# Pair products from tile 2 on, dense sums in place, six tile buffers in a ring, and two waits moved: one change to a fused attention and feed-forward kernel

## The chip, the cores and the metric

The kernel runs on one core of one Trainium2 chip. TensorE (PE) does the matmuls, VectorE (DVE), ScalarE (ACT) and GpSimd (POOL) the rest; SyncE (SP) issues nearly all transfers and POOL a few, and 16 DMA engines carry them. The metric is device time in microseconds for one execution; the output is checked against the reference, and smaller is better.

## The reference, cut to what matters

```python
x = L0_attn_inputs                       # (2, 1024, 1024), float32
x = x + attention(layernorm(x))          # conv of 3 taps to q, k, v (256 each), 16 heads of 64,
                                         # causal softmax in blocks of 128, wo, proj_w, proj_b
x = x + ffn(layernorm(x))

def ffn(x):                              # 2048 tokens, H = O = 1024, rank 8, 4 active experts of 16
    y = einsum('bth,oh->bto', x, W_base) + b_base
    z = einsum('bth,erh->bter', x, lora_A[active])
    contribs = einsum('bter,eor->bteo', z, lora_B[active]) * 2.0
    logits = (einsum('bth,eh->bte', x, router_W) + router_b)[..., active]
    alpha = softmax(log(domain_prior[active] + 1e-12) + logits)
    return y + einsum('bteo,bte->bto', contribs, alpha)
```

## The kernel before

It is one program in which each engine's instructions stand in an order written by hand, with semaphores between them. Every float32 product is done as three matmuls on a high and a low part (`three_pass`, L63 to L65). There are three stages: the convolution, the attention and the feed-forward part.

**Attention.** The 2048 tokens go in 8 groups of 256, each in 8 steps of two heads; two of these steps make one `attention_pair(D)`, so D runs from 0 to 32 and a group takes four of them. In pair D, TensorE does the scores of pair D-1, the head outputs of D-3, the turning of the softmax rows of D-2 (L1882, which waits for `p_ready`), and then queries and keys of D (at the start of a group these wait for `c_lo_ready`). GpSimd normalises the softmax rows (L722, which gives `p_ready`) and makes `c_lo` (L703); in every fourth pair it first adds the bias row to the residual rows `xr` (`bias_sum`, L713). The queries and keys come from `c_raw`, one buffer into which SP loads a group of 256 tokens (`load_c`, L480), and which ACT (`c_high`, L920) and GpSimd empty. SP issues transfers in the order of `attention_step(g, i)`: in step (0, 0) it gathers the gate weights of the four active experts (the list, then for each expert a register load and four small transfers, L607 to L614), in (0, 7) it loads group 2 of `c_raw`, in (1, 0) it loads the dense weights `fw_raw` (24 transfers, L618), and in (1, 3) the bias row `pb_r` and the first `xr`.

**Feed-forward.** 16 tiles of 128 tokens. The first `CL` = 4 are done plainly: `dense(t, b)` runs 8 chunks x 3 passes over three column blocks (1064 columns in all, 36 of them for gates and low rank), then three short matmuls add the low-rank part from `b_stack` (L2088), and DVE adds the sum to the tile's residual `x1t` and writes it to a buffer `y` of its own (`tile_outputs`, L1612), which POOL stores. The other 12 tiles go in 6 pairs of two tiles: seven products of half size in place of eight (`product`, L2039 to L2041, by the operands A11, S1, S2, A12, S3, A22, S4). Three of them use sums of weight blocks. These were formed in the attention stage, stored to memory, and come back in the feed-forward stage (`load_sums(kind)`, L567): kinds 0, 1 and 2 (each 8 transfers of 266 KB, into `t_v`, `t_p`, `t_b`, `t_f`) are for S1, S2 and S3, and kind 3 (8 of 266 KB into the right halves of `fw_hi` and `fw_lo`) is for A22. Kind 3 may only be loaded once the last plain tile is done with those columns (`y_done`), and each product's first matmul waits for its kind.

**Buffers.** Six buffers `x1t_0` to `x1t_5` hold residual tiles. `x1t_4` and `x1t_5` lie where `y` lies, so they are free only once the plain tiles are stored; `x_slot(t)` says which tile has which buffer. `x1g` holds a second, group-wise copy of a tile for its normalised and transposed operand (`load_groups(t)`, L539, four transfers of 128 KB, waits for `fturned`). Before the first dense tile, `b_raw` is split (ACT L1057, DVE L1704) and copied into `b_stack` by five transfers (L635); TensorE waits for these (`b_stacked`) ahead of the transpose of tile 0's gate columns (L2081).

Of the kernel before, what the change touches and what calls it, by code (L numbers as in the profile page):

```python
# [13 lines left out]
P = 128  # L14
# [73 lines left out]
def network(nc, ident, x, conv_w, conv_b, wq, wk, wv, wo, pw, bq, bk, bv, bo, pb, w_base, b_base, lora_a, lora_b, router_w, router_b,  # L88
# [70 lines left out]
    CL = 4  # L159
# [8 lines left out]
    XS = 4  # L168
# [14 lines left out]
    def x_slot(t):  # L183

        if t < CL:
            return t % XS
        h = CL // 2 % 2
        return 2 * (h, 1 - h, 2)[(t - CL) // 2 % 3] + t % 2

# [33 lines left out]
    with ExitStack() as ctx:  # L223
# [86 lines left out]
        y, = place(nc, XL + 2 * CHUNK, (("y", [P, 2, DM], F32),))  # L310
# [50 lines left out]
        y_stored = [sp.sem(f"y_stored{i}") for i in range(2)]  # L361
# [91 lines left out]
        def _(sync):  # L453
# [77 lines left out]
            def load_groups(t):  # L531

                if t < XS:
                    sync.wait_ge(s["a_step"], NJ)
                else:
                    sync.wait_ge(s["fturned"], 2 * (t - 1))
# [32 lines left out]
            def load_into_free(t):  # L569

                old = max((i for i in range(t) if x_slot(i) == x_slot(t)), default=None)
                if old is None:
                    for par in range(2):
                        sync.wait_ge(y_stored[par], 16 * (CL // 2))
                elif old < CL:
                    sync.wait_ge(s["y_ready"], NB * (old + 1))
# [5 lines left out]
            def attention_step(g, i):  # L582
# [22 lines left out]
                if (g, i) == (0, 0):  # L605
# [22 lines left out]
                if (g, i) == (9, 0):  # L628
                    load_groups(2)
# [28 lines left out]
            for t in range(XS, CL + 3):  # L658
                load_into_free(t)
                if t == XS:  # L660
                    load_sums(1)
                if t == (XS if CL == 2 else XS + 1):
                    load_sums(2)
                load_groups(t)
            load_groups(CL + 3)
            load_into_free(CL + 3)
# [12 lines left out]
        def _(pool):  # L679
# [79 lines left out]
            def store(t):  # L759
                pool.wait_ge(s["y_ready"], NB * (t + 1))  # L760
                pool.dma_start(out[t * P:(t + 1) * P], y[:, t % 2]).then_inc(y_stored[t % 2], 16)
# [28 lines left out]
            for q in range(NQ):  # L790
# [4 lines left out]
                if q:  # L795
                    store_pair(q - 1, 1)
            for par in range(2):
                pool.wait_ge(y_stored[par], 16 * (CL // 2))
# [4 lines left out]
        def _(act):  # L803
# [306 lines left out]
            if CL == 2:  # L1110
                tile_moments(CL)
            for t in range(CL):
# [7 lines left out]
                if t == CL - 2:  # L1120
                    tile_moments(CL + 1)
# [5 lines left out]
                if t == CL - 3:  # L1127
                    tile_moments(CL)
# [32 lines left out]
        def _(dve):  # L1161
# [299 lines left out]
            def tile_statistics(t):  # L1461
# [3 lines left out]
                dve.bn_stats(stats[:, par, 0], x1t[t % XS][:, 0:DM // 2])  # L1465
                dve.bn_stats(stats[:, par, 1], x1t[t % XS][:, DM // 2:DM]).then_inc(s["fstats_done"], 1)
# [720 lines left out]
```

## Time and profile before

| | |
|---|---|
| median of 3 runs | 777.4 us (776.33 to 778.8) |
| the profiled execution's own time | 777.63 us |
| its span | 775.9 us |
| TensorE busy | 752.0 us, 97% of the span |
| DVE, ACT, POOL busy | 553.0, 453.3, 172.0 us |
| HBM read, written | 82.68 MB, 34.80 MB |
| mean granted TensorE clock | 0.994 |

How to read it: times are microseconds from the start of the span. A row of the timeline has start, duration, engine, line, instruction, tiles, and in brackets how long the engine stood idle before it and what released it. SPq and POOLq are the queues of SP and POOL, so their rows are issues of transfers; the time that a transfer lands is its issue plus the time to landing. The granted clock is a share of TensorE's full speed of 2.4 GHz; 0.50 is 1.2 GHz. A busy TensorE is not one at its peak.

### The profile page before, as it was taken

The page shows a single profiled execution, that of the slowest core. Times are in us where ns is not written, and L with a number is a line of the kernel's source. Part 1 is how long each engine was busy: PE and PEld are TensorE (multiplying, and loading weights), DVE is VectorE, ACT ScalarE, POOL GpSimd, SP SyncE. Part 2 cuts the span into 40 slices and gives each one's busy share as a digit, 9 for nine tenths or more (in the row PEclk, how much of TensorE's full clock was granted, in tenths as well). Part 3 has the DMA queues.
Part 4 walks back from the last instruction along what each step waited for, and adds up shares of the span by engine and source line. Part 5 has one row for each costly group of instructions (what it writes and reads, how often), then busy time and mean ns, then how long its engine had stood idle before and what let it go on. Part 6 is the DMA issues. An engine that isn't in the chain of part 4 may idle for free.

```text
span 775.9 us, 15057 instructions
## 1 busy us (share of the span) xinstructions
PE 752.0 (97%) x5326; PEld 675.6 (87%) x5326; DVE 553.0 (71%) x1503; ACT 453.3 (58%) x1180; POOL 172.0 (22%) x204
## 2 busy tenths in 40 slices
PE   3999999999999998999999999999998999999997
PEld 3898888888888887989999989999987899999997
DVE  6999996889888864655656565466587657777874
ACT  5953442343434786777777777777791445666530
POOL 2300100000000222616162626252430111222200
PEclk9999999999999998999999999999999999999999
DMA  8846833444446139152516060603046967333502
GB/s 327 296 112 188 261 119 119 168 163 163 143 169 243 50 71 317 44 194 71 193 44 207 21 233 25 221 12 110 1 171 186 353 205 264 122 132 136 162 30 82
DMA packets 61246, 118.86 MB, mean 153 GB/s; under 512 B 11507, under 2 KB 30067, under 8 KB 59892
## 3 DMA queue, kind: packets, MB, share of 16 engines
q1 hardware_dynamic: 59156, 110.56, 42.9%
q0 software_dynamic: 2016, 7.34, 2.3%
q8 instruction: 43, 0.70, 0.4%
q14 instruction: 31, 0.25, 0.1%
HBM read 82.68 MB, written 34.80 MB: 151 GB/s over the span
## 4 chain that ended last, share of the span: by engine, by line
PE 89%; DVE 3%; ACT 3%; DMA 2%; SPq 2%; issue 1%; DVEq 0%; POOL 0%; ACTq 0%; POOLq 0%
PE net_psum L63 15%; PE net_psum L65 14%; PE net_psum L64 14%; PE net_psum L1797 11%; PE net_psum L2039 5%; PE net_psum L2041 5%; PE net_psum L2040 5%; PE net_psum L1859 4%; PE net_psum L1870 4%; PE net_psum L1882 4%; PE net_psum L1912 2%; PE net_psum L1913 2%; PE net_psum L1914 2%; PE net_psum L1781 1%; ACT pr L890 1%
## 5 line engine op out<-in xcount | busy, mean ns | idle before, releaser
L722 POOL TENSOR_TENSOR pr<-pr,rrec 128x512 f32<-128x512 f32 x64 | 66.6, 1042 | 215.1 <-DVE rrec L1333 212.5
L890 ACT ACTIVATE pr<-pr,negmax 128x128 f32<-128x128 f32 x256 | 99.0, 395 | 0.9 <-DVE negmax L1325 0.9
L1797 PE MATMUL net_psum<-ua,wa 128*128 128x256 f32 x384 | 83.8, 379 | 0.6 <-DVE ua L1215 0.6
L1797 PEld LDWEIGHTS net_psum<-ua,wa 128*128 128x128 f32 x384 | 72.6, 190 | 10.4 <-issue 0.8
L1325 DVE CUSTOM_DVE_ANT_0 pr<-net_psum,mask 128x128 f32<-128x128 f32 x256 | 57.1, 287 | 29.9 <-PE net_psum L1859 29.9
L63 PE MATMUL net_psum<-x_hi,w_hi 128*128 128x512 f32 x192 | 76.4, 398 | 0.0
L64 PE MATMUL net_psum<-x_lo,w_hi 128*128 128x512 f32 x192 | 76.2, 397 | 0.0
L65 PE MATMUL net_psum<-x_hi,w_lo 128*128 128x512 f32 x192 | 75.6, 394 | 0.0
L847 ACT ACTIVATE w_hi<-raw 128x1024 fp32r<-128x1024 f32 x24 | 25.5, 1061 | 85.2 <-PE net_psum L65 76.5
L63 PE MATMUL net_psum<-c_hi,wqk_hi 128*128 128x256 f32 x256 | 74.5, 291 | 0.0
L64 PE MATMUL net_psum<-c_lo,wqk_hi 128*128 128x256 f32 x256 | 71.8, 280 | 0.0
L65 PE MATMUL net_psum<-c_hi,wqk_lo 128*128 128x256 f32 x256 | 71.7, 280 | 0.0
L909 ACT ACTIVATE oT_hi<-net_psum,net_bv_c 128x256 fp32r<-128x256 f32 x64 | 26.9, 472 | 48.9 <-PE net_psum L1870 48.7
L1333 DVE RECIPROCAL rrec<-rsum 128x4 f32<-128x4 f32 x64 | 11.4, 178 | 58.0 <-ACT pr L890 57.9
L64 PEld LDWEIGHTS net_psum<-c_lo,wqk_hi 128*128 128x128 f32 x256 | 48.5, 190 | 1.3
L890 ACT ACTIVATION_READ_ACCUMULATOR pr<-pr,negmax 128x1 f32 x256 | 49.6, 194 | 0.0
L63 PEld LDWEIGHTS net_psum<-c_hi,wqk_hi 128*128 128x128 f32 x256 | 48.4, 189 | 1.3
L65 PEld LDWEIGHTS net_psum<-c_hi,wqk_lo 128*128 128x128 f32 x256 | 48.3, 189 | 0.0
L65 PEld LDWEIGHTS net_psum<-x_hi,w_lo 128*128 128x128 f32 x192 | 36.3, 189 | 8.6
L63 PEld LDWEIGHTS net_psum<-x_hi,w_hi 128*128 128x128 f32 x192 | 35.9, 187 | 8.9
L64 PEld LDWEIGHTS net_psum<-x_lo,w_hi 128*128 128x128 f32 x192 | 36.2, 188 | 8.5
L1605 DVE TENSOR_TENSOR x1t<-net_psum,x1t 128x528 f32<-128x528 f32 (+1 forms) x48 | 32.1, 689 | 15.7 <-PE net_psum L2041 14.6
(268 smaller groups left out, 2260.9 us busy)
## 6 DMA issues: line engine op xcount, KB each, us to landing
wa<-in_conv_w SPq DMA_DIRECT2D x24, 512.0 KB, 3.9
raw<-in_conv_w SPq DMA_DIRECT2D x24, 384.0 KB, 4.2
xn<-in_x SPq DMA_DIRECT2D x16, 512.0 KB, 10.2
xr<-in_x SPq DMA_DIRECT2D x8, 1024.0 KB, 5.5
x_scratch<-xr SPq DMA_DIRECT2D x8, 1024.0 KB, 4.4
x1t<-x_scratch SPq DMA_DIRECT2D x16, 512.0 KB, 4.7
x1g<-x_scratch SPq DMA_DIRECT2D x56, 128.0 KB, 3.0
c_raw<-c_scratch SPq DMA_DIRECT2D x7, 768.0 KB, 5.3
```

The source lines that it names most:

```text
L63: pe.matmul(out, w_hi, x_hi, start=first, stop=False)
L64: pe.matmul(out, w_hi, x_lo, start=False, stop=False)
L65: return pe.matmul(out, w_lo, x_hi, start=False, stop=last)
L722: pool.tensor_tensor(pr[:, jj % 4], pr[:, jj % 4], rrec[:, jj % 4].unsqueeze(2).to_broadcast([P, UN, P]), ALU.mult).then_inc(s["p_ready"], 1)
L890: e = act.activation(pr[:, jj % 4, un], pr[:, jj % 4, un], ACT.Exp, bias=negmax[:, jj % 2, un:un + 1], scale=-1.0, accum_out=rsum[:, jj % ...
L1325: m = dve.tensor_tensor_reduce(out=pr[:, jj % 4, un], in0=scp[:, h, jj % 2 * GT + b * P:jj % 2 * GT + (b + 1) * P], in1=mask[:], scale=-DH ...
L1605: dve.tensor_tensor(half_of(tile, j), bank_half(b, j), half_of(tile, j), ALU.add).then_inc(s["y_ready"], 1)
L1797: mm = pe.matmul(duo_acc(d, mi)[:, v * QUADS:(v + 1) * QUADS], wa[:, a % AW, mi, 1 - v, c % 2], ua[:, c, v, n * QUADS:(n + 1) * QUADS], st ...
L1859: mm = pe.matmul(scp[:, h, o], qf[e, jj % 2, t], kf[e, jj % 2, t], start=True, stop=True)
L2039: pe.matmul(to, x_hi, b_hi, start=c == 0 and o in (A11, S1, A12), stop=False, skip_group_check=True)
L2040: pe.matmul(to, x_hi, b_lo, start=False, stop=False, skip_group_check=True)
L2041: mm = pe.matmul(to, x_lo, b_hi, start=False, stop=c == DC // 2 - 1, skip_group_check=True)
```

## The change

`CL` goes from 4 to 2: tiles 0 and 1 are dense, and tiles 2 to 15 go in 7 pairs. The plain tiles' sums are written over `x1t` itself, `y` is gone, and the tiles take the six buffers in turn (`t % 6`). SP loads tiles 4 and 5 once the heads are done (`o_done`), ahead of the group copies of tiles 2 and 3, and the three kinds of weight sums follow each other with nothing between. The gather of the gate weights moves from step (0, 0) to (0, 7), behind the load of group 2. `b_lo` is computed one DVE instruction earlier, and TensorE's wait for `b_stack` goes from the transpose to the first matmul that reads it. ACT takes the moments of tiles 2 and 3 before the first turn of gate columns.

```diff
     NB = 3
-    CL = 4
+    CL = 2
     NQ = (TT - CL) // 2
...
-        if t < CL:
-            return t % XS
-        h = CL // 2 % 2
-        return 2 * (h, 1 - h, 2)[(t - CL) // 2 % 3] + t % 2
+        return t % len(x1t)
...
-                old = max((i for i in range(t) if x_slot(i) == x_slot(t)), default=None)
-                if old is None:
-                    for par in range(2):
-                        sync.wait_ge(y_stored[par], 16 * (CL // 2))
+                old = t - len(x1t)
+                if old < 0:
+                    sync.wait_ge(s["o_done"], NJ)
                 elif old < CL:
-                    sync.wait_ge(s["y_ready"], NB * (old + 1))
+                    sync.wait_ge(y_stored[old // 2], 32)
                 else:
...
                     load_tile(1)
-                if (g, i) == (0, 0):
+                if (g, i) == (0, 7):
                     sync.wait_ge(s["unit_done"], NK)
...
                 if (g, i) == (9, 0):
+                    load_into_free(4)
+                    load_into_free(5)
                     load_groups(2)
...
             load_sums(0)
-            for t in range(XS, CL + 3):
-                load_into_free(t)
-                if t == XS:
-                    load_sums(1)
-                if t == (XS if CL == 2 else XS + 1):
-                    load_sums(2)
+            if CL > 2:
+                load_groups(4)
+            load_sums(1)
+            load_sums(2)
+            for t in range(5 if CL > 2 else 4, CL + 4):
+                if t >= len(x1t):
+                    load_into_free(t)
                 load_groups(t)
-            load_groups(CL + 3)
-            load_into_free(CL + 3)
             load_sums(3)
...
                 pool.wait_ge(s["y_ready"], NB * (t + 1))
-                pool.dma_start(out[t * P:(t + 1) * P], y[:, t % 2]).then_inc(y_stored[t % 2], 16)
+                pool.dma_start(out[t * P:(t + 1) * P], x1t[x_slot(t)][:]).then_inc(y_stored[t // 2], 16)
...
-            if CL == 2:
-                tile_moments(CL)
+            act.wait_ge(s["tables_ready"], 4 + 2 * TG)
+            tile_moments(CL)
+            tile_moments(CL + 1)
             for t in range(CL):
...
                     gate_exponential(t)
-                if t == CL - 2:
-                    tile_moments(CL + 1)
                 if t == CL - 1:
                     pair_scale(0, 1)
                 gate_turned(t)
                 if t == 0:
                     tile_xT(t + 1)
-                if t == CL - 3:
-                    tile_moments(CL)
             high_operand(0, A11)
...
                 dve.wait_ge(s["y_done"], NB * t + b + 1)
-                if b == 0:
-                    wait(dve, y_stored[t % 2], 16 * (t // 2))
                 lo, hi = OUT[b]
-                dve.tensor_tensor(y[:, t % 2, lo:hi], yp[t % 2][b][:, OFF[b]:OFF[b] + hi - lo], x1t[x_slot(t)][:, lo:hi], ALU.add).then_inc(s["y_ready"], 1)
+                tile = x1t[x_slot(t)][:, lo:hi]
+                dve.tensor_tensor(tile, yp[t % 2][b][:, OFF[b]:OFF[b] + hi - lo], tile, ALU.add).then_inc(s["y_ready"], 1)
...
             last_bias(1)
-            unit_out(ND + 3, 0)
             dve.wait_ge(s["b_split_hi"], 1)
             dve.tensor_tensor(b_lo[:], b_raw[:], b_hi[:], ALU.subtract).then_inc(s["b_split_lo"], 1)
+            unit_out(ND + 3, 0)
             unit_out(ND + 3, 1)
...
                 if t == 0:
-                    pe.wait_ge(s["b_stacked"], 16 * 5)
                     pe.wait_ge(s["a_lo_ready"], NG)
...
                 pe.wait_ge(s["azsT_ready"], t + 1)
+                if t == 0:
+                    pe.wait_ge(s["b_stacked"], 16 * 5)
                 for b in range(NB):
```

SP's queue at the start of the attention, before. `c_raw` is the group load, `act_sb` the list of experts, `a_raw`, `r_raw` and `lbias` the gathers (those of the other three experts repeat these rows and are left out), `fw_raw` the dense weights:

```order
L654 DMA c_scratch<-cyz 128x1536
L607 DMA act_sb<-in_active 1x4
L610 TENSOR_LOAD act_sb
L611 DMA a_raw<-in_lora_a 128x8x8
L612 DMA r_raw<-in_router_w 128x8
L613 DMA lbias<-in_router_b 128x1
L614 DMA lbias<-in_prior 128x1
...
L480 DMA c_raw<-c_scratch 128x6x256
L618 DMA fw_raw<-in_w_base 128x248
```

and in the changed kernel:

```order
L650 DMA c_scratch<-cyz 128x1536
L475 DMA c_raw<-c_scratch 128x6x256
L601 DMA act_sb<-in_active 1x4
L604 TENSOR_LOAD act_sb
...
L608 DMA lbias<-in_prior 128x1
L612 DMA fw_raw<-in_w_base 128x248
```

The load of `c_raw` has changed places with the whole gather; the dense weights, and the loads of `pb_r` and `xr` after them, still follow the gather.

SP's queue from the group copies of tiles 2 and 3 to the right halves of the weights, before (with buffer numbers; rows of one kind of sum that go on alike are left out):

```order
L539 DMA x1g_0_170<-x1_scratch 32x4x256 x4
L539 DMA x1g_1_171<-x1_scratch 32x4x256 x4
...
L586 DMA x1_scratch<-xr_140 128x2x1024
L567 DMA t_v0_183<-t_scratch 128x532
...
L529 DMA x1t_0_145<-x1_scratch 128x1024
L567 DMA t_v8_191<-t_scratch 128x532
...
L539 DMA x1g_0_170<-x1_scratch 32x4x256 x4
L529 DMA x1t_1_146<-x1_scratch 128x1024
L567 DMA t_p3_199<-t_scratch 128x532
...
L529 DMA x1t_3_154<-x1_scratch 128x1024
L567 DMA fw_hi_158<-t_scratch 128x532 x4
```

and in the changed kernel:

```order
L524 DMA x1t_4_156<-x1_scratch 128x1024
L524 DMA x1t_5_157<-x1_scratch 128x1024
L534 DMA x1g_0_170<-x1_scratch 32x4x256 x4
...
L580 DMA x1_scratch<-xr_140 128x2x1024
L562 DMA t_v0_182<-t_scratch 128x532
...
L562 DMA t_f0_205<-t_scratch 128x532
L534 DMA x1g_0_170<-x1_scratch 32x4x256 x4
L534 DMA x1g_1_171<-x1_scratch 32x4x256 x4
L562 DMA fw_hi_158<-t_scratch 128x532 x4
L562 DMA fw_lo_151<-t_scratch 128x532 x4
```

Four tile loads are gone from among the sums and two stand ahead of everything; two group copies, of tiles 4 and 5, now stand between the last sum and the right halves.

TensorE at tile 0's gate columns, with the semaphores that each waits for, before:

```order
L2081 MATMUL net_psum<-ident,azs 98x128 [waits net_azs_ready,net_a_lo_ready,net_b_stacked]
L1951 MATMUL net_psum<-ident,fxn_159 128x128 [waits net_xT_lo_ready,net_fxn_ready]
L63 MATMUL net_psum<-fw_hi,xT_hi 128x264 [waits net_oT_lo_ready]
...
L2088 MATMUL net_psum<-b_stack,azsT 128x248 [waits net_azsT_ready]
```

and in the changed kernel:

```order
L2072 MATMUL net_psum<-ident,azs 98x128 [waits net_azs_ready,net_a_lo_ready]
L1943 MATMUL net_psum<-ident,fxn_159 128x128 [waits net_xT_lo_ready,net_fxn_ready]
L63 MATMUL net_psum<-fw_hi,xT_hi 128x264 [waits net_oT_lo_ready]
...
L2081 MATMUL net_psum<-b_stack,azsT 128x248 [waits net_b_stacked,net_azsT_ready]
```

The wait for `b_stacked` stands behind the transposes of tile 1 and the 24 matmuls of tile 0's last column block.

## Rows read from the trace of the kernel before

**Rows 1.** The page: busy time of the engines, share of the span, instructions.
```profile
PE 752.0 (97%) x5326; PEld 675.6 (87%) x5326; DVE 553.0 (71%) x1503; ACT 453.3 (58%) x1180; POOL 172.0 (22%) x204
```
**Rows 2.** Waits of TensorE: line, who is waited for, us in total, times, longest.
```profile
PE net_psum L1859 <- ACT kf L899: 3.3, 1, 3.3
PE net_psum L2081 <- DMA b_stack<-b_lo: 2.1, 1, 2.1
```
**Rows 3.** Chain of waits: ends of plain tiles 2, 3 (L2088) and pairs 1, 2 (L2065).
```profile
624.10 0.47 PE net_psum L2088 x3
...
636.56 0.47 PE net_psum L2088 x3
...
680.77 0.47 PE net_psum L2065 x4
...
703.00 0.47 PE net_psum L2065 x4
```
**Rows 4.** Timeline of SP's queue, start of the attention.
```profile
271.46 0.33 SPq L607 DMA_DIRECT2D act_sb<-in_active  x1
...
287.77 0.39 SPq L480 DMA_DIRECT2D c_raw<-c_scratch  x1
288.22 14.14 SPq L618 DMA_DIRECT2D fw_raw<-in_w_base  x24
...
302.87 0.43 SPq L591 DMA_DIRECT2D xr<-in_x  x1
```
**Rows 5.** Timelines of DVE, ACT and TensorE: `c_raw` of group 1, the stall behind group 2.
```profile
273.46 1.81 DVE L1375 TENSOR_TENSOR c_lo<-c_raw,c_hi 128x768 fp32r<-128x768 f32 x2
...
293.38 0.84 ACT L920 ACTIVATE c_hi<-c_raw 128x768 fp32r<-128x768 f32 x1 [3.17 <-DMA c_raw<-c_scratch]
...
297.27 1.22 PE L1859 MATMUL net_psum<-kf,qf 64*128 64x128 f32 x8 [3.26 <-ACT kf L899]
```
**Rows 6.** Stretches: length, busy PE, PEld, DVE, ACT, POOL, granted clock, DMA share, GB/s.
```profile
297.00:303.00 6.00, 5.73 (x37) 5.18 (x38) 3.82 (x19) 3.20 (x6) 0.09 (x1) 0.50 1.04 357
...
593.00:596.00 3.00, 0.96 (x10) 0.96 (x10) 2.25 (x5) 0.45 (x2) 0.51 (x1) 1.00 0.61 194
```
**Rows 7.** Timelines of GpSimd and TensorE, D = 7 and 8.
```profile
312.10 4.79 POOL L713 TENSOR_TENSOR xr<-xr,pb_r 128x1024 f32<-128x1024 f32 x2
316.86 1.04 POOL L722 TENSOR_TENSOR pr<-pr,rrec 128x512 f32<-128x512 f32 x1
319.40 1.82 POOL L703 TENSOR_TENSOR c_lo<-c_raw,c_hi 128x768 fp32r<-128x768 f32 x1
...
321.81 1.09 PE L1882 MATMUL net_psum<-ident,pr 128*128 128x128 f32 x8
```
**Rows 8.** Issues from 302 to 303.5: count, KB each, us to landing.
```profile
xr<-in_x SPq DMA_DIRECT2D x1, 1024.0 KB, 8.4
```
**Rows 9.** Timelines of DVE, ACT and SP's queue ahead of tile 0; a small transfer's landing.
```profile
589.47 1.21 DVE L1704 TENSOR_TENSOR b_lo<-b_raw,b_hi 33x1024 fp32r<-33x1024 f32 x1
...
595.39 0.28 ACT L1108 ACTIVATE azsT<-net_psum 98x128 fp32r<-98x128 f32 x1 [9.34 <-PE net_psum L2081]
...
594.61 5.04 SPq L567 DMA_DIRECT2D t_v<-t_scratch  x8
...
b_stack<-b_lo SPq DMA_DIRECT2D x1, 4.0 KB, 1.7
```
**Rows 10.** Timeline of TensorE: first matmuls of pair 0 and of its product A22.
```profile
636.88 0.28 PE L2039 MATMUL net_psum<-fw_hi,xT_hi 128*128 128x266 f32 x1
...
651.97 0.30 PE L2039 MATMUL net_psum<-fw_hi,xT_hi 128*128 128x266 f32 x1
```
**Rows 11.** Stretches of the feed-forward stage, columns as in rows 6.
```profile
600.00:612.00 12.00, 12.00 (x77) 10.82 (x76) 7.68 (x25) 4.00 (x9) 1.70 (x2) 1.00 1.02 381
612.00:624.00 12.00, 12.00 (x77) 10.88 (x77) 6.30 (x20) 4.11 (x9) 2.98 (x9) 1.00 1.05 343
642.00:648.00 6.00, 6.00 (x52) 6.00 (x51) 3.48 (x6) 3.28 (x7) 1.65 (x6) 1.00 1.04 402
```

More of the change, by code:

```diff
@@ L167, in network @@
     SOON = 2
-    XS = 4
     TG = 4
@@ L309, in network @@
                    + [part[:, k // 2, DC // 2 * (k % 2):DC // 2 * (k % 2) + DC // 2] for k in range(2, 4)] for i, part in enumerate((xT_hi, xT_lo))]
-        y, = place(nc, XL + 2 * CHUNK, (("y", [P, 2, DM], F32),))
         b_raw, b_hi, b_lo, b_stack = place(nc, XH, (("b_raw", [ER + 1, DM], F32), ("b_hi", [ER + 1, DM], F32R), ("b_lo", [ER + 1, DM], F32R),
@@ L360, in network @@
         xg_loaded = [sp.sem(f"xg_loaded{i}") for i in range(2)]
-        y_stored = [sp.sem(f"y_stored{i}") for i in range(2)]
+        y_stored = [sp.sem(f"y_stored{i}") for i in range(CL // 2)]
         block = ctx.enter_context(nc.Block())
@@ L531, in load_groups @@
             def load_groups(t):
-                if t < XS:
+                if t < 4:
                     sync.wait_ge(s["a_step"], NJ)
@@ L796, in _ @@
                     store_pair(q - 1, 1)
+            for stored in y_stored:
+                pool.wait_ge(stored, 32)
             for par in range(2):
-                pool.wait_ge(y_stored[par], 16 * (CL // 2))
                 pool.wait_ge(pair_stored[par], 32 * len(range(par, NQ - 1, 2)))
@@ L1464, in tile_statistics @@
                 wait(dve, s["fmv_done"], t - 1)
-                dve.bn_stats(stats[:, par, 0], x1t[t % XS][:, 0:DM // 2])
-                dve.bn_stats(stats[:, par, 1], x1t[t % XS][:, DM // 2:DM]).then_inc(s["fstats_done"], 1)
+                dve.bn_stats(stats[:, par, 0], x1t[x_slot(t)][:, 0:DM // 2])
+                dve.bn_stats(stats[:, par, 1], x1t[x_slot(t)][:, DM // 2:DM]).then_inc(s["fstats_done"], 1)
             def variance(t):
@@ L1481, in tile_scale @@
                     dve.wait_ge(s["pT_done"], NJ)
-                dve.tensor_scalar(fxn[par][:].rearrange("p (j i d) -> p i j d", i=TG, j=DC), x1t[t % XS][:].rearrange("p (i j d) -> p i j d", i=TG, j=DC), mv[:, par, 0:1], rstd[:, par], ALU.subtract, ALU.mult).then_inc(s["fxn_ready"], 1)
+                dve.tensor_scalar(fxn[par][:].rearrange("p (j i d) -> p i j d", i=TG, j=DC), x1t[x_slot(t)][:].rearrange("p (i j d) -> p i j d", i=TG, j=DC), mv[:, par, 0:1], rstd[:, par], ALU.subtract, ALU.mult).then_inc(s["fxn_ready"], 1)
             def low_xT(t):
```

## The prediction

> **What bounds the kernel now.** Read the page first: TensorE is busy in 97% of the span, DVE in 71% [rows 1]. Nothing off TensorE's path pays, and a gain is either less work for it or a wait taken away. So the waits of TensorE come next. Past the start only two are large: 3.3 us in the attention, behind ACT, and 2.1 us ahead of tile 0, behind the transfers of `b_stack` [rows 2]. The first has a longer story. ACT stood 3.17 us for `c_raw` of group 2, which SP issued only at 287.77 because the gather of the gate weights, from 271.46 on, stood ahead of it; TensorE then waited until 297.27 [rows 4, 5]. Afterwards the granted clock was 0.50, that is 1.2 GHz, over 297 to 303, with TensorE busy 5.73 us of it [rows 6]. At full clock that work takes half, so the stall cost 3.26 + 2.87 = 6.1 us. The 2.1 us wait did not do this: over 593 to 596 the clock stayed at 1.00 [rows 6].
>
> **Two tiles become a pair.** From the end of plain tile 2 to that of tile 3 it is 636.56 - 624.10 = 12.46 us, so two plain tiles are 24.92; from pair to pair it is 703.00 - 680.77 = 22.23 [rows 3]. Gain 2.7 us of TensorE time. What DVE, ACT and POOL do for a pair hides today in that same 22.23 and needs nothing new. The first pair starts behind a plain tile, as now. ACT's moments of tiles 2 and 3 fall in the 9.34 us in which it now stands idle before the first turn of gate columns [rows 9]; without that cover the four activations would hold up tile 1's operand by a few microseconds.
>
> **Sums in place.** The same three additions, written elsewhere; the loads of tiles 4 and 5 go ahead of the group copies, where the engines are hardly used. I cost them at nothing; they relieve a crowded stretch, below.
>
> **The wait for `b_stack`.** TensorE is free 2.1 us before `b_stack` lands [rows 2]. The wait now stands behind eight transposes and 24 matmuls of 264 columns. Five products of 24 matmuls of 266 columns take 651.97 - 636.88 = 15.1 us, so 24 are 3.0 us [rows 10]. Even with today's landing nothing is left of the wait. `b_lo` goes ahead of one evacuation, which it delays by at most its own 1.21 us [rows 9]; the bank behind that is wanted later, so I take 0 and keep 0.3 for it. Gain 2.1 us (2.05 in the sum).
>
> **The gather.** Removed: the stall of group 2, 6.1 us. `c_lo` of group 1 ends at 273.46 + 1.81 = 275.3 [rows 5]; there `c_raw` of group 2 goes out, and it is wanted 15 us later. But every instruction of the gather is now in front of a later start. It takes 287.77 - 271.46 = 16.3 us, so it ends at about 292.0 instead of 287.8. Behind it are 24 loads of `fw_raw` (14.1 us), `pb_r` and `xr`: `xr` is issued at about 306.7 instead of 302.87 [rows 4]. It took 8.4 us to land [rows 8], 311.3, just ahead of GpSimd's `bias_sum` at 312.10 [rows 7]: that wait is hidden today and no longer will be, since all else comes 6.1 us earlier. `c_raw` (768 KB, 0.79 MB) is out of the backlog, which at 357 GB/s [rows 6] is 2.2 us, so I have `xr` land at 306.7 + 6.2 = 312.9. Behind `bias_sum` (4.79 us) GpSimd has two normalisations of 1.04 and `c_lo` of group 2, 1.82 [rows 7]: the first softmax rows at 318.7, `c_lo` at 312.9 + 8.7 = 321.6. TensorE wants these rows at 321.81 - 6.1 = 315.7 and the queries and keys of group 2 one microsecond on. They start at 321.6 rather than, as now, at 321.81 + 1.02 = 322.8. Of 6.1 us only 1.2 are left; TensorE idles 3.0 us, then in pieces to 4.9 in all. Such an idle pulled the clock down at 3.26 us and did not at 2.1 [rows 5, 6]. I take it as falling again. It costs 2.87 if the whole of the low stretch is work and half of that if half of it is spent in these waits; I take 2.0. Attention stage: -1.2 + 2.0 = 0.8 us slower. Bounds: `xr` no earlier than its bytes allow, 5.77 MB (`fw_raw`, `pb_r`, `xr`) at the best rate, 402 GB/s [rows 11], after 292.0, that is 306.4, which gives back all 6.1; and no later than 306.7 + 8.4 = 315.1, which makes it 1.0 slower, with the clock 3.9.
>
> **The weight sums come earlier.** Pair 0 now starts at 636.88 - 24.92 - 2.05 = 609.9, and its product A22, which needs the right halves (kind 3), at +15.1 = 625.0 [rows 10]. SP starts with the sums at 594.61 as now, 0.63 us an issue [rows 9], so 24 are issued by 609.7 and issuing is not the limit. The engines are: from 600 on their share is over 1 [rows 11]. In their queue stand the last store of `xr` (1.05 MB), 24 sums (6.54) and the store of tile 0 (0.52): 8.11 MB at 381 GB/s, 21.3 us. Then the group copies of tiles 4 and 5 (1.05) with the store of tile 1 (0.52) at the slower 343, 4.6 us; then kind 3, 2.18 MB at 402, 5.4 us [rows 11]. With 1.7 us from issue to landing of a small transfer [rows 9] the right halves are there at 594.6 + 1.7 + 31.3 = 627.6. By the same count S1, S2 and S3 find their sums in time (S3 wants them 10.5 us after the start, at 620.4; 594.6 + 1.7 + 21.3 = 617.6). So TensorE waits 2.6 us at A22. It is a new wait in place of a gain. Bounds: all 11.86 MB at 402 is 29.5 us, 625.8, and less where POOL's second store is not ahead of kind 3, so 0; all at 343 is 34.6, 630.9, so 5.9. What is late next, the group copies, hides behind it.
>
> The Trainium skill says (DMA: Bandwidth & Descriptors, "Where 436 GB/s comes from") that between HBM and SBUF a core gets about 358 GB/s, the HBM side binding. By that the 11.86 MB would take 33.1 us and A22 wait 4.4 us, which would speak against the change. The trace does not keep to it: 381 and 402 GB/s over 12 and 6 us [rows 11]. The same page ("Queues, rings and completion order") has each DMA engine go round the queues that have work, so that POOL's stores take their share ahead of SP's backlog; that is why I count the store of tile 1 before kind 3. Without it the wait would be 1.3 us.
>
> **Sum.** Feed-forward: -2.69 - 2.05 + 2.6 = -2.1. Attention: +0.8. Together -1.3 us against the profiled execution's 777.63, whose median of runs is 777.4: 776.1 us.
>
> **Rivals.**
> 1. *Slower: the right halves come later and the clock falls there too.* One mechanism, at A22 of pair 0. For it: the queue has 31 us of work and 30 us of room, and the lower rate of the stretch, 343 GB/s, is a measured one. Against it: 2.6 us is nearer to the 2.1 that left the clock alone than to the 3.3 that did not. It decides from a wait of about 3.3 us. With 3.5 us of wait and 2.87 of clock the stage is -4.74 + 6.4 = +1.6, in all +2.4: 779.8 us; with the full bound 782.
> 2. *The sums are in time.* At 402 GB/s throughout, the wait is 0.8 us or none, the stage -3.9 to -4.7, the whole about 773.9 (777.4 - 4.3 + 0.8). For it: 402 GB/s was held over the 6 us in which kind 3 came before. Against it: the queue also holds stores and small-row copies, and the rate dips with them [rows 11].
> 3. *The attention keeps its gain.* `xr` lands by 310, as its bytes alone would allow, or the clock holds in GpSimd's broken waits. Then that stage is -1.2 to -4 instead of +0.8: 771.3 to 774.1, taken at 773. For it: SP's 14.1 us for `fw_raw` may have been stretched by the backlog behind `c_raw`. Against it: `xr` is issued after all of them whatever the engines do.
>
> **Chances.** The forecast 0.42, own range 774.3 to 778; rival 1 0.18; rival 2 0.18; rival 3 0.18; the remaining 0.04 is for both gains at once, 770. A difference under 0.3% (2.3 us) cannot be told from none. Faster by more: rivals 2 and 3 and the last case mostly, 0.34, with 0.08 from the lower end of the forecast: 0.42. Within: the rest of the forecast and the lower half of rival 1, 0.43. Slower by more: 0.15. Range 770.8 to 780.3; it leaves out all gains at once and rival 1's far end.
>
> **What the changed kernel's profile would show.** The wait on `c_raw` at group 2 gone and ACT not idle before `c_hi`; GpSimd idle before `bias_sum` on the transfer of `xr`, with TensorE waiting for `pr` and `c_lo` in D = 8 and a clock of 0.50 after it; no wait for `b_stack`; seven pairs of 22.2 us; a wait of 2 to 4 us of A22's first matmul on `fw_hi` or `fw_lo` from memory, once. The prediction is wrong if TensorE never waits in D = 8, if the first pair runs without a gap, or if the clock falls in neither place or in both.

## The result, and the profile after

| | before | changed |
|---|---|---|
| median of 4 runs each | 777.45 us (776.33 to 778.8) | 783.12 us (781.96 to 784.15) |
| ratio, 95% interval | | 1.0069 (1.0052 to 1.0086) |
| profiled execution, its span | 777.63, 775.9 us | 781.96, 780.2 us |
| mean granted TensorE clock | 0.994 | 0.989 |

The changed kernel is 5.4 us slower by the ratio (4.0 to 6.7); the forecast was 776.1, and 783.1 lies outside its range. The profiled execution, the fastest of its four, is 4.3 us longer in its span.

First the page, its line of busy times. TensorE's is nearly that of [rows 1].

```profile
PE 752.3 (96%) x5350; PEld 677.9 (87%) x5350; DVE 553.2 (71%) x1494; ACT 463.7 (59%) x1200; POOL 172.9 (22%) x210
```

That time counts low-clock matmuls at their longer duration, so 752.3 against 752.0 does not mean that the pair saved nothing. The waits of TensorE, columns as in [rows 2], the whole list over 0.5 us:

```profile
PE net_psum L1773 <- ACT xn L812: 10.8, 3, 9.8
PE net_psum L2031 <- issue: 6.4, 1, 6.4
PE net_psum L1874 <- POOL pr L717: 3.3, 1, 3.3
PE net_psum L63 <- POOL c_lo L698: 0.7, 1, 0.7
PE net_psum L1789 <- DVE ua L1208: 0.6, 1, 0.6
PE net_psum L1851 <- DVE kf L1347: 0.6, 1, 0.6
```

Both waits of [rows 2] are gone. In their place are 3.3 + 0.7 us behind GpSimd in the attention, and 6.4 us at one matmul of the feed-forward stage.

**Attention.** SP's queue, to be held against [rows 4]:

```profile
275.36 0.37 SPq L475 DMA_DIRECT2D c_raw<-c_scratch  x1
275.77 0.44 SPq L601 DMA_DIRECT2D act_sb<-in_active  x1
280.93 0.69 SPq L605 DMA_DIRECT2D a_raw<-in_lora_a  x1
...
293.21 11.50 SPq L612 DMA_DIRECT2D fw_raw<-in_w_base  x24
...
305.24 0.43 SPq L585 DMA_DIRECT2D xr<-in_x  x1
```

`c_raw` goes out 12.4 us earlier and `xr` 2.4 us later. The timeline of GpSimd and TensorE, against [rows 7], and two stretches behind it (columns as in [rows 6]):

```profile
313.60 4.66 POOL L708 TENSOR_TENSOR xr<-xr,pb_r 128x1024 f32<-128x1024 f32 x2 [7.38 <-DMA xr<-in_x]
318.21 2.10 POOL L717 TENSOR_TENSOR pr<-pr,rrec 128x512 f32<-128x512 f32 x2
319.31 2.17 PE L1874 MATMUL net_psum<-ident,pr 128*128 128x128 f32 x8 [3.29 <-POOL pr L717]
320.28 1.81 POOL L698 TENSOR_TENSOR c_lo<-c_raw,c_hi 128x768 fp32r<-128x768 f32 x1
...
322.14 0.58 PE L63 MATMUL net_psum<-c_hi,wqk_hi 128*128 128x256 f32 x1 [0.66 <-POOL c_lo L698]
```

```profile
312.00:320.00 8.00, 4.71 (x50) 4.13 (x49) 3.94 (x9) 1.82 (x6) 6.40 (x4) 0.95 0.03 12
320.00:326.00 6.00, 5.34 (x22) 4.40 (x21) 3.43 (x20) 2.08 (x5) 2.09 (x2) 0.50 0.43 123
```

GpSimd stands 7.38 us for `xr`, and TensorE, which needs the rows that GpSimd normalises behind it, stands too; over 320 to 326 its clock is 0.50. DVE's normalisation of tile 0, which ends the stage, starts at 582.30 and started at 581.05 before: 1.25 us later.

**Feed-forward.** SP's queue from the last store of `xr` on:

```profile
594.88 0.39 SPq L580 DMA_DIRECT2D x_scratch<-xr  x1
595.37 8.58 SPq L562 DMA_DIRECT2D t_v<-t_scratch  x13
...
609.22 0.55 SPq L562 DMA_DIRECT2D t_f<-t_scratch  x1
609.82 6.86 SPq L534 DMA_DIRECT2D x1g<-x_scratch  x8
616.72 2.04 SPq L562 DMA_DIRECT2D fw_hi<-t_scratch  x4
619.12 2.29 SPq L562 DMA_DIRECT2D fw_lo<-t_scratch  x4
626.86 4.11 SPq L534 DMA_DIRECT2D x1g<-x_scratch  x8
```

The same time by stretches, and the first matmul of A22 in TensorE's timeline:

```profile
596.00:600.00 4.00, 4.00 (x33) 3.95 (x32) 1.98 (x5) 1.31 (x4) 0.16 (x1) 1.00 0.99 309
600.00:604.00 4.00, 4.00 (x25) 3.59 (x24) 2.36 (x10) 2.39 (x7) 0.62 (x1) 1.00 1.03 344
604.00:618.00 14.00, 14.00 (x102) 13.23 (x102) 9.65 (x18) 9.53 (x18) 2.65 (x7) 1.00 1.04 401
618.00:626.00 8.00, 8.00 (x66) 7.89 (x64) 2.57 (x5) 2.45 (x6) 1.06 (x3) 1.00 1.09 273
626.00:630.00 4.00, 0.14 (x2) 0.00 (x0) 3.42 (x5) 2.40 (x5) 0.00 (x0) 0.98 1.06 378
...
630.00:636.00 6.00, 3.42 (x15) 3.46 (x16) 3.15 (x13) 0.91 (x3) 0.00 (x0) 0.50 1.12 226
```

```profile
632.58 0.56 PE L2031 MATMUL net_psum<-fw_hi,xT_hi 128*128 128x266 f32 x1 [6.44 <-issue]
```

The 16 engines are busy throughout (share 0.99 and more), but what they move falls from 401 to 273 GB/s over 618 to 626. The group copies `x1g` of tiles 4 and 5 go through from 618 to 624, and the first part of kind 3 behind them. The last of kind 3 (`fw_lo`) is issued by 621.4. A22 is wanted at 626.1 and starts at 632.58. The clock falls to 0.50 while TensorE stands there and stays down over the first 4 us of its work. The waits list says "issue" because the profile does not see which semaphore ended it: A22's first matmul waits for kind 3, for its operand (made by 620) and for DVE's addition of product S3, which ended at 627.4; only the transfers come later than that. By the trace's packet records the last packet of kind 3 ended at 631.5. In each of the eight kernels of this document whose A22 wait is put down to "issue", A22 starts 0.9 to 1.3 us behind that packet.

### The profile page after: what moved, and what is told of

The parts are those of the page before. It is cut to its first block, busy times and chain, and to the rows that moved or that the text cites. A ratio compares the mean times of both kernels' runs of the same rounds, so it can differ in the third digit from the quotient of the medians.

```text
span 780.2 us, 15138 instructions
## 1 busy us (share of the span) xinstructions
PE 752.3 (96%) x5350; PEld 677.9 (87%) x5350; DVE 553.2 (71%) x1494; ACT 463.7 (59%) x1200; POOL 172.9 (22%) x210
## 4 chain that ended last, share of the span: by engine, by line
PE 83%; SPq 5%; DMA 3%; DVE 3%; issue 2%; ACT 2%; POOL 1%; DVEq 0%; ACTq 0%; POOLq 0%
PE net_psum L63 13%; PE net_psum L64 12%; PE net_psum L65 12%; PE net_psum L1789 11%; PE net_psum L2031 6%; PE net_psum L2033 6%; PE net_psum L2032 6%; PE net_psum L1851 4%; PE net_psum L1862 3%; PE net_psum L1874 3%; SPq L562 2%; PE net_psum L1904 2%; PE net_psum L1905 2%; PE net_psum L1906 2%; SPq L612 1%
## 5 line engine op out<-in xcount | busy, mean ns | idle before, releaser
L2031 PE MATMUL net_psum<-fw_hi,xT_hi 128*128 128x266 f32 x168 | 49.9, 297 | 6.4 <-issue 6.4
L1598 DVE TENSOR_TENSOR x1t<-net_psum,x1t 128x528 f32<-128x528 f32 (+1 forms) x56 | 37.4, 688 | 19.1 <-PE net_psum L2033 16.8
L2032 PE MATMUL net_psum<-fw_lo,xT_hi 128*128 128x266 f32 x168 | 48.8, 291 | 0.0
L2033 PE MATMUL net_psum<-fw_hi,xT_lo 128*128 128x266 f32 x168 | 48.8, 291 | 0.0
```

What stands on the lines that cost most here:

```text
L1598: dve.tensor_tensor(half_of(tile, j), bank_half(b, j), half_of(tile, j), ALU.add).then_inc(s["y_ready"], 1)
L2031: pe.matmul(to, x_hi, b_hi, start=c == 0 and o in (A11, S1, A12), stop=False, skip_group_check=True)
L2032: pe.matmul(to, x_hi, b_lo, start=False, stop=False, skip_group_check=True)
L2033: mm = pe.matmul(to, x_lo, b_hi, start=False, stop=c == DC // 2 - 1, skip_group_check=True)
```

## The experiments

Five rounds each, beside the kernel before on the same chip. Differences in microseconds are the ratio times 777.4. The last two columns are of the one profiled execution of each kernel.

| kernel | median us | ratio (95%) | A22's wait | tile 0 normalised at |
|---|---|---|---|---|
| changed | 783.12 | 1.0069 (1.0052 to 1.0086) | 6.4 | 582.30 |
| a_gather_back | 780.48 | 1.0034 (1.0023 to 1.0045) | 6.4 | 578.94 |
| b_gather_late | 778.62 | 1.0026 (1.0014 to 1.0038) | none | 581.75 |
| b_gather_xr | 772.80 | 0.9932 (0.9919 to 0.9945) | none | 574.86 |
| a_gather_xr | 774.91 | 0.9972 (0.9962 to 0.9982) | 6.3 | 574.90 |
| a_sums_first | 784.03 | 1.0080 (1.0067 to 1.0093) | 8.2 | 582.69 |
| a_sums_first2 | 784.09 | 1.0088 (1.0074 to 1.0103) | 1.7, then 6.4 | 582.58 |
| a_stores_late | 781.90 | 1.0051 (1.0037 to 1.0064) | 6.7 | 582.16 |
| a_small_copies | 777.04 | 0.9994 (0.9985 to 1.0004) | 2.3 | 583.38 |
| a_long_rows | 782.41 | 1.0065 (1.0051 to 1.0079) | 6.2 | 580.83 |
| a_wide2 | 781.62 | 1.0055 (1.0041 to 1.0069) | 4.9 | 582.66 |
| a_cl4 | 776.20 | 0.9989 (0.9980 to 0.9998) | none | 582.05 |
| a_cl4_xr | 769.32 | 0.9897 (0.9881 to 0.9912) | none | 575.10 |
| b_best | 770.05 | 0.9903 (0.9888 to 0.9918) | none | 575.10 |

**The gather alone, taken out and put in.** In the changed kernel back to step (0, 0); in the kernel before to (0, 7):

```diff
-                if (g, i) == (0, 7):
+                if (g, i) == (0, 0):
```

> The changed kernel with the gather of the gate weights back in step (0, 0); all else as changed. Theory (the feed-forward stage carries the loss: A22 of pair 0 waits 6.4 us for kind 3 and the clock falls, in all +3.3; the gather costs only +1.0 to +1.2): the stall of 3.3 us behind c_raw of group 2 comes back, xr is on time again, and the time is the changed kernel's 783.1 less 1.1, about 782.0, which is +4.5 over the kernel before. A22's wait stays at 6 to 6.5 us. Rival (the late gather carries the loss): about 777.4 to 778.

> The kernel before with only the gather moved from step (0, 0) to (0, 7). Theory: the wait on c_raw of group 2 goes, but xr lands at 313.6, GpSimd waits 7.4 us for it, TensorE 3.3 + 0.7 us in D = 8 with a clock of 0.50 behind it; 777.45 + 1.1 = 778.5 us. Rival (the late gather carries the loss of the changed kernel): 782 to 783. Rival (the forecast's third: the attention keeps its gain): 773.

Put in, it costs 2.0 us (1.1 to 3.0); taken out, it gives back 2.7. The rest of the loss, 2.6 us (1.8 to 3.5), stands in a_gather_back with an early gather, and A22's wait with it. So the loss has two parts of about one size; neither rival holds. The attention's share was put at 1.1 and is nearer 2. The price of an early gather differs from one execution to the next: a_gather_back's trace is of the fastest of its ten executions, 2.4 us under their median, and the stall of [rows 5] was 2.4 us in it and not 3.3.

**The first `xr` ahead of the gather**, in the kernel before (where the gather goes to step (0, 7) as well) and in the changed one:

```diff
                     sync.wait_ge(s["unit_done"], NK)
+                    sync.dma_start(pb_r[:], ...)
+                    sync.dma_start(xr[:], x_rows(..., 0))
                     sync.dma_start(act_sb[:], active)
...
-                        if g == 1:
-                            sync.dma_start(pb_r[:], ...)
-                        wait(sync, s["x1_stored"], 16 * (g - 1))
-                        sync.dma_start(xr[:], x_rows(..., g - 1))
+                        if g > 1:
+                            wait(sync, s["x1_stored"], 16 * (g - 1))
+                            sync.dma_start(xr[:], x_rows(..., g - 1))
```

> The kernel before with the gather in (0, 7), and the loads of the bias row pb_r and of the first xr issued there too, ahead of the gather instead of behind the 24 weight loads. Theory (a late xr is all that eats the gain in the attention): c_raw of group 2 and xr are both in time, GpSimd does not wait, TensorE has no wait over 1 us in D = 7 and 8 and no clock of 0.50 there: 777.45 - 6.1 = 771.3 us. Rival (the stall's price was over-read: the clock falls for another reason, or something behind is late next): 774 or more.

> The changed kernel with pb_r and the first xr ahead of the gather. Theory (the two parts of the loss are separate; in the kernel before the same edit took a late gather from 778.6 to 772.8): the waits in D = 8 go, A22's wait of 6.4 us stays: 783.1 - 5.8 = 777.3 us, the same as the kernel before. Rival (the attention's end earlier makes the feed-forward stage wait more): 779 or more.

GpSimd's timeline of b_gather_xr, to be held against the 7.38 us above:

```profile
303.21 2.81 POOL L704 TENSOR_TENSOR c_lo<-c_raw,c_hi 128x768 fp32r<-128x768 f32 x1
305.99 4.76 POOL L714 TENSOR_TENSOR xr<-xr,pb_r 128x1024 f32<-128x1024 f32 x2
310.81 1.04 POOL L723 TENSOR_TENSOR pr<-pr,rrec 128x512 f32<-128x512 f32 x1
```

No wait for `xr`, none of TensorE in D = 7 and 8. Tile 0 is normalised at 574.86 and not 581.05: 6.2 us, which is the price that the prediction gave the stall (6.1). At the end of the span 4.7 of them are left. The same wait for `b_stack` as in [rows 2] stands in this trace, and here the clock fell behind it, which in the kernel before it did not [rows 6]:

```profile
588.85 0.31 PE L2082 MATMUL net_psum<-ident,azs 128*98 128x128 f32 x1 [2.08 <-DMA b_stack<-b_lo]
```

```profile
590.00:592.00 2.00, 2.00 (x11) 2.00 (x10) 1.46 (x3) 0.84 (x2) 0.00 (x0) 0.50 1.02 260
```

By the clocks of 588 to 594 (0.89, 0.50 and 0.76 over 2 us each) some 3.4 us of work went at half speed, which is an estimate of 1.7 us lost; so this, too, differs between executions, and the 1.5 us that the expectation of 771.3 missed are likely of this kind. By the ratios the kernel is 5.3 us under the kernel before and 7.3 under b_gather_late; in the changed kernel the same edit gives 7.5. The two agree, and A22's wait stays as it was (6.3), so the two losses are separate. The 5.8 us of the expectation was a difference of medians, and the median of b_gather_late lies low in its ten runs (778.06 to 781.35).

**Kind 3 ahead of the group copies of tiles 4 and 5.** If A22 waits because kind 3 stands behind them, the order should cure it:

```diff
-            for t in range(5 if CL > 2 else 4, CL + 4):
-                if t >= len(x1t):
-                    load_into_free(t)
-                load_groups(t)
             load_sums(3)
+            for t in range(4, CL + 4):
+                load_groups(t)
```

> The changed kernel with the sums of kind 3 issued ahead of the group copies of tiles 4 and 5. Theory (kind 3 is late because it stands behind 1.05 MB of group copies that drain at some 240 GB/s, 4.4 us): the last sum before it lands at 621.3; 2.18 MB at 400 GB/s are there 5.4 us behind, 626.7 to 627.5, so A22 waits 0.7 to 1.5 us in place of 6.4 and the clock holds (another -2). The group copies land some 5.5 us later, tile 5's at about 631, and then scaling 2.1, transpose 1.25 and four operations of 0.7 stand ahead of pair 1's operands, so up to 2 us may come back at pair 1. Time 783.1 - 6.9 + 0 to 2 = 776.2 to 778.2, taken at 777. Rival (the queue is simply too full, whatever the order: pair 1 waits as long as A22 did): 781 to 783.

No gain at all, and a wait of 8.2 us at the same matmul. Timeline of ACT, DVE and TensorE in a_sums_first:

```profile
630.59 4.04 ACT L1074 ACTIVATE x1g<-x1g,gs 128x256 f32<-128x256 f32 x8 [8.45 <-DMA x1g<-x_scratch]
632.75 1.24 DVE L1556 STREAM_TRANSPOSE fxT<-x1g 128x1024 f32<-128x1024 f32 x1 [11.10 <-ACT x1g L1074]
633.92 0.67 DVE L1596 TENSOR_TENSOR x1t<-net_psum,x1t 128x528 f32<-128x528 f32 x1
...
634.64 0.59 PE L2029 MATMUL net_psum<-fw_hi,xT_hi 128*128 128x266 f32 x1 [8.16 <-DVE x1t L1596]
```

Read from the bottom: A22 may overwrite its bank only once DVE has added product S3 out of it. In DVE's order that addition stands behind the transposition of tile 4's copy, that behind ACT's scaling, and that behind the transfer, now last in the queue. The kernel a_sums_first2 keeps this order of the queue and puts the addition first:

```diff
+                if q == 0:
+                    pair_sum(q, 4)
                 if more:
                     pair_turn(q + 1, 0)
-                pair_sum(q, 4)
+                if q:
+                    pair_sum(q, 4)
```

> The changed kernel with the sums of kind 3 ahead of the group copies of tiles 4 and 5, as before, and with DVE adding the product S3 of pair 0 into its tile ahead of the transposition of tile 4's copy (TensorE's A22 may only overwrite that bank once it is added, and with the copies late it stood 8.2 us behind that transposition). Theory (the stretch as a whole is short of transfer time: whatever is loaded last is waited for): A22 waits 1 to 2 us, until kind 3 lands at about 628; pair 1 is wanted at 634 and has its operand at 637.8, so it waits 3.8 us and the clock falls: about 782 us. Rival (the loss was the order alone): pair 1 waits under 1 us, 777.

The waits of TensorE in a_sums_first2:

```profile
PE net_psum L2047 <- DVE azs L1547: 6.4, 1, 6.4
...
PE net_psum L2032 <- issue: 1.7, 1, 1.7
```

A22 waits 1.7 us, as forecast from kind 3's landing, and the rest comes a product later: TensorE stands 6.4 us at the turn of tile 2's gates (L2047), whose DVE work stands behind the two transpositions. It was looked for at pair 1 with 3.8 us; the place was wrong and the size too low, the verdict is the same. Nothing is won by the order, since by the end of pair 0 everything in this queue is needed.

**What in the queue costs so much.** Three quarters of those copies left out (32 rows of 1 KB a transfer, not 128):

```diff
-                for i in range(TG):
-                    sync.dma_start(x1g[...][i * 32:(i + 1) * 32], rows[:, :, ...])
+                n = 1 if t in (4, 5) else TG
+                for i in range(TG):
+                    sync.dma_start(x1g[...][i * 32:(i + 1) * 32, 0:n], rows[:, 0:n, ...])
```

> The changed kernel with three quarters of the group copies of tiles 4 and 5 left out (each of their eight transfers brings 32 rows of 1 KB in place of 128; those tiles' outputs are wrong). Theory (each packet takes an engine some 80 ns whether it has 1 or 2 KB, so the 1024 packets of 1 KB of these copies cost 1024 x 80 / 16 = 5.1 us of the queue, twice what their bytes would at 400 GB/s): 768 packets less are 3.8 us, A22 waits 2.6 us in place of 6.4, the clock may hold. With it held the time is 783.1 - 3.8 - 2 = 777.3, otherwise 779.3. Rival (the copies cost what their bytes do): 0.79 MB at 400 GB/s is 2.0 us, A22 waits 4.4, the time is 781.

The outputs of tiles 4 and 5 are wrong in this kernel and in the next two; they are for the timing alone. A22 waits 2.3 us (4.1 less for 0.79 MB less), the clock holds, and 5.8 us are back: all of the loss in the feed-forward stage and more.

```profile
629.42 0.36 PE L2032 MATMUL net_psum<-fw_hi,xT_hi 128*128 128x266 f32 x1 [2.27 <-issue]
```

0.79 MB in 4.1 us is 190 GB/s, half the queue's rate. The length of the rows, or the 32 partitions that each transfer writes? Same bytes, same eight transfers: whole rows of 4 KB into 32 partitions, then rows of 1 KB into 128.

```diff
+  # a_long_rows, tiles 4 and 5
+  sync.dma_start(x1g[...][i * 32:(i + 1) * 32]..., x1[t * P + i * 32:t * P + (i + 1) * 32])
+  # a_wide2, tiles 4 and 5
+  sync.dma_start(x1g[...][:, g], x1[t * P + 32 * g:t * P + 32 * (g + 1)].rearrange("q (i d) -> (q i) d", i=TG))
```

> The changed kernel with the group copies of tiles 4 and 5 read as whole rows: the same eight transfers of 128 KB into 32 partitions each, but 32 packets of 4 KB in place of 128 of 1 KB (the wrong elements for these two tiles, whose outputs are wrong). Theory (the length of a packet decides, not the 32 partitions): the copies drain at about 400 GB/s, 2.6 us for the 1.05 MB in place of 5.1, so A22 waits 3.9 us in place of 6.4: 780.6 us. Rival (it is the 32 partitions that one transfer writes to): the rate stays at 200 to 240 GB/s, A22 waits 6.4 us, 783.

> The changed kernel with the group copies of tiles 4 and 5 done as 128 rows of 1 KB into all 128 partitions, in place of 4 x 32 rows of 1 KB into 32 partitions; still eight transfers of 128 KB (wrong elements for these two tiles, whose outputs are wrong). Theory A (what slows these copies is that all 16 engines write to 32 partitions at once; whole rows of 4 KB into 32 partitions took 273 ns a packet against 160 into 128): the packets of 1 KB take 40 to 50 ns in place of 80, the copies drain in 2.6 to 3.3 us in place of 5.1, A22 waits 4 to 5 us in place of 6.4, and the time is 1.5 to 2.5 us under the changed kernel's, about 781. Theory B (a packet costs 80 ns up to 2 KB wherever it goes): A22 waits 6.4 us still, 783.

One stretch of 2 us while the copies drain, in the changed kernel, in a_long_rows and in a_wide2 (the last two columns are DMA share and GB/s):

```profile
620.00:622.00 2.00, 2.00 (x18) 1.98 (x17) 1.22 (x2) 0.18 (x1) 0.00 (x0) 1.00 1.14 237
```

```profile
618.00:620.00 2.00, 2.00 (x18) 1.92 (x16) 1.31 (x2) 0.00 (x0) 0.00 (x0) 1.00 1.05 231
```

```profile
620.00:622.00 2.00, 2.00 (x18) 2.00 (x18) 1.31 (x2) 0.11 (x1) 0.00 (x0) 1.00 1.11 362
```

```profile
631.36 0.46 PE L2034 MATMUL net_psum<-fw_hi,xT_hi 128*128 128x266 f32 x1 [4.94 <-issue]
```

The mean time of a packet, by the traces' packet records, says it more sharply:

| packets | into | mean ns | kernel |
|---|---|---|---|
| 2128 B (weight sums) | 128 partitions | 87 | changed, 606 to 612 |
| 4096 B (tile 1's store) | from 128 | 160 | changed, 616 to 618 |
| 1024 B (group copies) | 32 partitions | 77 | changed, 620 to 622 |
| 4096 B | 32 partitions | 282 | a_long_rows, 618 to 622 |
| 1024 B | 128 partitions | 49 | a_wide2, 620 to 622 |

So the slow rate comes with the 32 partitions, not with the short rows: the theory of a_long_rows fell, and so did theory B of a_wide2. Long rows brought 0.2 us of A22's wait, wide ones 1.5. But with no slow copy left ahead of kind 3, A22 still waits 4.9 us; the 32 partitions explain a part of the wait only. By the runs a_wide2 is 1.1 us under the changed kernel, within the intervals. A wide form that brings the right elements was not run.

**Stores out of the way.** GpSimd's stores of tiles 0 and 1 issued only behind kind 3:

```diff
-                store(t)
             for q in range(NQ):
...
+                if q == 0:
+                    pool.wait_ge(t_loaded[3], 16 * 8)
+                    store(0)
+                    store(1)
```

> The changed kernel with GpSimd's stores of tiles 0 and 1 (1.05 MB) issued only once the sums of kind 3 have landed. Theory (the queue of transfers between 595 and 631 is what A22 waits for, and every byte ahead of kind 3 counts alike): 1.05 MB at 400 GB/s is 2.6 us, A22 waits 3.8 us, the clock falls still: 780.5 us. Rival (stores to memory go beside the loads at no cost to them): A22 waits 6.4, 783.

A miss: 1.05 MB less ahead of kind 3, and A22 waits 6.7 us. The time is 1.4 us lower, inside the intervals. By the packet records the bulk of kind 3 did come earlier: of its 1024 packets 991 had begun by 628, against 731 in the changed kernel. But the last 33 begin only over 628 to 632, among the copies of tiles 6 and 7 that SP issues from 625.4 on, and the very last begins at 631.4 in both kernels. Some engines seem to be late while others go on to what is next; since the records do not name the engine, that is argued, not shown. No run keeps the copies of tiles 6 and 7 back until kind 3 has landed, so what makes the last packets late stays open.

**The two plain tiles back, all else as changed**, without and with the early `xr`:

```diff
-    CL = 2
+    CL = 4
```

> The changed kernel with CL = 4 again: four plain tiles and six pairs, and all else as changed (sums in place, six buffers in turn, SP's new order, the late gather, the moved wait). Theory (the feed-forward stage loses only because the pairs begin two plain tiles earlier, 25 us, on the same queue of transfers): A22 of pair 0 does not wait, the wait for b_stack is gone, the late gather costs its 1 to 2 us: 777.4 + 1.1 to 2.0 - 2.05 = 776.5 to 777.3 us. Rival (the new buffers or the new order of the loads lose by themselves): 780 or more.

> The same with pb_r and the first xr ahead of the gather. Theory: as the kernel before with the same edits of the attention and of b_stack, which took 770.05 us; in place and six buffers change nothing at CL = 4: 770. Rival (the tiles loaded ahead of the group copies relieve something): 769 or less. Rival (they crowd the start of the stage): 772 or more.

Both near the theory's times, 0.3 and 0.7 us under them. The sums in place, the six buffers, SP's new order and the moved wait lose nothing that these runs can tell; in the feed-forward stage only the earlier start of the pairs does. The waits of TensorE in a_cl4_xr, the whole list over 0.3 us:

```profile
PE net_psum L1774 <- ACT xn L813: 11.3, 4, 9.7
PE net_psum L1852 <- DVE kf L1348: 0.6, 1, 0.6
PE net_psum L1790 <- DVE ua L1209: 0.6, 1, 0.6
```

**The kernel before with the edits of the attention and of `b_stack`:** the gather in step (0, 7), `pb_r` and the first `xr` ahead of it, as above, and

```diff
-            unit_out(ND + 3, 0)
             dve.wait_ge(s["b_split_hi"], 1)
             dve.tensor_tensor(b_lo[:], b_raw[:], b_hi[:], ALU.subtract).then_inc(s["b_split_lo"], 1)
+            unit_out(ND + 3, 0)
...
-                    pe.wait_ge(s["b_stacked"], 16 * 5)
...
                 pe.wait_ge(s["azsT_ready"], t + 1)
+                if t == 0:
+                    pe.wait_ge(s["b_stacked"], 16 * 5)
```

> The kernel before (four plain tiles, six pairs) with the late gather, pb_r and the first xr ahead of it, and the two edits on b_stack: b_lo one DVE instruction earlier, TensorE's wait at the first matmul that reads it. Theory: the gather part gave 4.8 us by itself (772.8); the wait of 2.1 us for b_stack goes, with nothing in its place: 772.8 - 2.05 = 770.8. Rival (the waiting only moves to the weight sums or to the group copies of the first pair): 772 to 773.

770.05 us, by the ratios 2.3 us less than b_gather_xr: the `b_stack` wait was worth its 2.05, and a little more where the clock falls behind it. This kernel and a_cl4_xr are 7.5 and 8.0 us under the kernel before.

## Why the prediction was wrong, point by point

1. **Pair for two plain tiles, -2.69.** Right. The critical chain ends pairs 22.21 us apart (from 662.92 to 685.13 at L2057), as in [rows 3].
2. **Sums in place, six buffers, 0.** Right: a_cl4 is 0.9 us under the kernel before, and -2.05 for `b_stack` with +1 to 2 for the gather make just that.
3. **The wait for `b_stack`, -2.05.** Right: gone, nothing in its place; b_best against b_gather_xr says 2.3.
4. **The gather, +0.8.** Right in its links, low in size: the stall went, `xr` came at 313.6 (forecast 312.9), GpSimd and TensorE stood in D = 8 for 4.0 us (4.9) and the clock fell. It came to +1.25 in the profiled execution, 2.0 (1.1 to 3.0) by the runs. SP's part ended 1.2 us later than worked out, 293.2 and not 292.0: the list of experts, now issued behind 768 KB of `c_raw`, took 5.2 us to come and not 3.9. The 24 weight loads, at 11.5 us, gave more than that back, and yet `xr` landed 0.7 us later than forecast. The stall's price was not fixed either (2.4 us of wait in a_gather_back), and the clock fell behind `b_stack` in b_gather_xr and not in the kernel before; "did not at 2.1" held in the traces of the kernel before and of b_gather_late, and not in that one.
5. **"So TensorE waits 2.6 us at A22": this is the step that failed.** It waits 6.4, beyond the upper bound of 5.9, and the clock then falls, which the forecast had hold: (6.4 - 2.6) + 2 = 5.8 us too few (4 us of work at half speed, 632.6 to 636.7, are the 2). The bytes were right, and so was the time for the first part: 309, 344 and 401 GB/s over 596 to 600, 600 to 604 and 604 to 618 make 8.2 MB by 618, where the prediction had 8.11 by 617.6. Behind that two terms failed, and A22 starts at 632.6 and not at 627.6.
   - *The rate behind 618*, "the group copies of tiles 4 and 5 with the store of tile 1 at the slower 343" and kind 3 at 402. That is 3.0 MB by 626; 2.2 MB went. At 402 GB/s the difference is 1.9 us. The 343 GB/s is an average over 12 us of which the copies are a small part [rows 11], 0.64 of 4.1 MB; cut finer, the trace of before had the slow rate in it already:

```profile
614.00:616.00 2.00, 2.00 (x15) 1.89 (x14) 1.91 (x4) 0.00 (x0) 1.29 (x5) 1.00 1.10 235
620.00:622.00 2.00, 2.00 (x15) 1.76 (x14) 0.00 (x0) 0.85 (x3) 1.10 (x4) 1.00 1.05 403
```

   It is 237 in the changed kernel while the copies drain. a_wide2, where they drain at 362, brings 1.5 us of the wait back. Kind 3's first packets are slowed with them: 144 ns over 623 to 625, against 87.
   - *The end of kind 3*, for which the forecast had nothing. At 626 some 1.4 MB of it were left, 3.5 us at 402 GB/s; A22 starts 6.6 us later. Of the 3.1 us more, about 1 lies between the last packet's end and the matmul. The other 2 are the last packets' own: 36 of the 1024 begin only behind 629.5, the last at 631.4, among the copies of tiles 6 and 7. In a_stores_late fewer bytes stood ahead and the last packets came no earlier; what makes them late stays open.

   The two make 5.0 us; A22 was wanted 1.1 us later than forecast (626.1, not 625.0), which leaves the 3.8 us by which the wait was too short. The bound "all at 343" was no bound: it knew neither of the two.
6. **The rivals.** Rival 1 named this mechanism with 0.18 and a far end of 782; it is what happened, and a bit worse. The Trainium skill's 358 GB/s between HBM and SBUF (DMA: Bandwidth & Descriptors, "Where 436 GB/s comes from") would have given a wait of 4.4 us and so come nearer, but not for its reason: the trace shows 401 GB/s over 604 to 618, 14 us. Another line of that page was passed over, "Rules for kernel authors", which wants 128 partitions for the highest bandwidth; the trace agrees, 49 ns against 77 for the same 1 KB.
7. **The sum.** -2.69 - 2.05 + 6.4 + 2 is +3.7 for the feed-forward stage, where the profiled execution shows 3.05 (4.3 less 1.25); with 1.25 to 2.0 of the attention that is 4.9 to 5.7, and the measured loss is 5.4. CL = 2 by itself costs 5.8 us (a_gather_xr 0.9972 against a_cl4_xr 0.9897).

## What to carry to other kernels

An average rate over a stretch is no rate for the one kind of transfer that decides: cut the stretch until it holds that kind alone, and let the upper bound be the slowest such piece. Where less compute stands in front of a fixed queue of loads, add up the queue against the new time that is left for it; if it does not fit, changing the order only moves the wait. And a transfer moved to an earlier place is worth its price only if what stood behind it in that queue, here the first `xr`, moves with it.

## What the runs showed of the hardware that was not expected

- Transfers that write into 32 partitions moved 237 GB/s with all engines busy where their rows had 1 KB (77 ns a packet, changed kernel, 620 to 622), 231 where they had 4 KB (282 ns, a_long_rows), and as little as 168 over 625 to 627 in a_sums_first. Into 128 partitions it was 49 ns for 1 KB, 87 ns for 2128 B, and 160 ns for 4 KB out of them.
- The end of a group of transfers can take long when others are queued behind it: the last 33 of kind 3's 1024 packets took from 628 to 631.4 in a_stores_late.
- Under 1 KB rows into 128 partitions the queue still moved 362 GB/s.
- TensorE's clock does not follow from the length of one wait. Behind the same wait of 2.1 us for `b_stack` it held in the kernel before and fell to 0.50 in b_gather_xr. It held after waits of 2.3 us (a_small_copies) and 1.7 (a_sums_first2); it fell after 6.4, 6.3, 4.9 and 3.3, and also after one of 2.4 us in a_gather_back, where it was 0.72 over 296 to 300.
- At 0.50 it stayed down for 4 us of A22's work after a wait of 6.4 us.
